# Addresses at multiples of 2048 bytes and two steps moved: a two-layer graph kernel in split fp32 on one NeuronCore

## What is computed

```
x1  = layernorm(x + adj @ (scale * (adj @ (x @ W0))) + bias)
deg1 = row sums of adj, deg2 = row sums of adj.T   (0 replaced by 1)
out = layernorm(x1 + (adj / deg1) @ x1 @ W_in + (adj.T / deg2) @ x1 @ W_out)
scale = sum over levels of d_list * filt * d_list
```

## Time and profile before

| | |
|---|---|
| median of 3 runs | 754.64 us (754.17 to 755.70) |
| profiled execution, its own time | 754.41 us |
| its span, first to last instruction | 752.6 us |
| TensorE busy | 740.1 us, 3337 matmuls |
| VectorE busy | 552.9 us |
| ScalarE busy | 475.0 us |
| mean granted TensorE clock | 0.998 |
| HBM read, written | 205.95 MB, 2.10 MB |

### The profile page before, as it was taken

How to read it: one execution, slowest core, us unless ns; L and a number is a source line. 1 busy time by engine, 2 the same in 40 slices (tenths; PEclk the granted TensorE clock), 3 DMA queues, 4 the chain that set the end, 5 groups by cost and what they waited for, 6 DMA issues and landing times. The chain is left out here.

```text
span 752.6 us, 9059 instructions
## 1 busy us (share of the span) xinstructions
PE 740.1 (98%) x3337; PEld 605.5 (80%) x3337; DVE 552.9 (73%) x673; ACT 475.0 (63%) x1167; POOL 0.2 (0%) x4
## 2 busy tenths in 40 slices
PE   8999999999999999999999999999999999999995
PEld 5878888888888888788888888888887888888884
DVE  4896865838373464787665647988679999899994
ACT  5996673837263543234343446998799888877771
POOL 0000000000000000000000000000000000000000
PEclk9999999999999999999999999999999999999999
DMA  9998875656656445255455459999989999999981
GB/s 325 411 375 342 356 264 214 258 215 209 216 191 223 168 168 224 78 209 207 178 175 217 167 197 373 381 385 381 382 303 371 384 366 373 381 358 336 348 350 29
DMA packets 35532, 208.64 MB, mean 277 GB/s; under 512 B 3616, under 2 KB 8480, under 8 KB 11040
## 3 DMA queue, kind: packets, MB, share of 16 engines
q1 hardware_dynamic: 35072, 207.86, 73.5%
q10 hardware_dynamic: 416, 0.20, 0.1%
HBM read 205.95 MB, written 2.10 MB: 276 GB/s over the span
## 5 line engine op out<-in xcount | busy, mean ns | idle before, releaser
L376 DVE TENSOR_TENSOR lo<-raw,hi 128x2048 fp32r<-128x2048 f32 x184 | 417.0, 2287 | 139.4 <-ACT hi L274 104.6
L274 ACT ACTIVATE hi<-raw 128x512 fp32r<-128x512 f32 x512 | 315.5, 620 | 60.8 <-DMA raw<-in_adjT_b 38.4
L575 PE MATMUL accA<-hi,x_hi 128*128 128x512 f32 x512 | 203.1, 397 | 1.4 <-ACT x_hi L282 0.7
L578 PE MATMUL accA<-hi,x_lo 128*128 128x512 f32 x512 | 200.3, 391 | 0.3 <-DVE x_lo L381 0.3
L277 ACT ACTIVATE hi<-raw 128x2048 fp32r<-128x2048 f32 x64 | 121.7, 1912 | 72.1 <-DMA raw<-in_adjT_b 72.1
L584 PE MATMUL accA<-lo,x_hi 128*128 128x512 f32 x512 | 138.5, 392 | 0.8 <-DVE lo L376 0.8
L575 PEld LDWEIGHTS accA<-hi,x_hi 128*128 128x128 f32 x512 | 96.2, 188 | 23.1 <-ACT hi L274 2.0
L584 PEld LDWEIGHTS accA<-lo,x_hi 128*128 128x128 f32 x512 | 95.9, 188 | 22.8 <-DVE lo L376 1.7
L578 PEld LDWEIGHTS accA<-hi,x_lo 128*128 128x128 f32 x512 | 96.2, 188 | 20.8 <-DVE x_lo L381 0.6
L575 PE MATMUL accB<-hi,v_hi 128*128 128x512 f32 x256 | 101.2, 395 | 0.9 <-DVE turned L433 0.9
L578 PE MATMUL accB<-hi,v_lo 128*128 128x512 f32 x256 | 100.1, 391 | 0.0
(11 more groups left out here) (66 smaller groups left out, 461.4 us busy)
## 6 DMA issues: line engine op xcount, KB each, us to landing
raw<-in_adjT_b SPq DMA_DIRECT2D x127, 1024.0 KB, 4.9
raw<-in_adj_b SPq DMA_DIRECT2D x64, 1024.0 KB, 5.0
rows<-in_xT_b SPq DMA_DIRECT2D x8, 256.0 KB, 9.8
rows<-in_x_t SPq DMA_DIRECT2D x8, 256.0 KB, 5.9
out<-rows SPq DMA_DIRECT2D x7, 256.0 KB, 5.6
raw<-in_adjT_b SPq DMA_DIRECT2D x4, 256.0 KB, 5.0
out<-rows SPq DMA_DIRECT2D x1, 128.0 KB, 1.9
out<-rows ACTq DMA_DIRECT2D x1, 128.0 KB, 1.9
```

The lines of the kernel that those rows point to most:

```text
L274: nc.scalar.activation(hi[slot][:, t], raw[slot][:, t], ACT.Copy, accum_out=sums[:, TPB * K + t, C:C + 1]).then_inc(s_hi, 1)
L376: nc.vector.tensor_tensor(lo[slot][:], raw[slot][:], hi[slot][:], ALU.subtract).then_inc(s_lo, 1)
L575: nc.tensor.matmul(acc, r_hi[:, TPB * K + t], h[:, t], start=(first and t == 0), stop=False)
L578: nc.tensor.matmul(acc, r_lo[:, TPB * K + t], h[:, t], start=False, stop=False)
```

## The change

1. The ring is placed at a multiple of 2048 bytes in place of 64, so it starts at 129,024 and no longer at 131,008. A tensor `unused` of 1920 bytes is put ahead of x_hi, which then starts at 18,432 in place of 16,512; x_lo, v_hi, v_lo, each 16,384 bytes, and all that comes after follow.
2. turn_z(7) on ScalarE and v_block(7) on VectorE are done in iteration N1 and no longer in N1 + 1.
3. In iteration N1 + 3 VectorE does o_sum(6) between x1_block(7) and x1_parts(7).

```diff
+LINE = 4 * BLK
...
-        ring_at = nc.sbuf_top // 64 * 64 - 2 * RING * CHUNK
+        ring_at = nc.sbuf_top // LINE * LINE - 2 * RING * CHUNK
...
+        pair_at = -(-nc.sbuf_base // LINE) * LINE
+        sb("unused", [P, (pair_at - nc.sbuf_base) // 32 * 8])
         x_hi = sb("x_hi", [P, NT, P], F32R)
...
                 if 0 <= I < NB - 1 and n < N1 + 2:
                     turn_z(I)
-                if n == N1 + 1:
+                if n == N1:
                     turn_z(NB - 1)
...
-                if n == N1 + 1:
+                if n == N1:
                     v_block(NB - 1)
                 if n == N1 + 2:
                     o_sum(NB - 1)
                 if n == N1 + 3:
                     x1_block(NB - 1)
+                    o_sum(NB - 2)
                     x1_parts(NB - 1)
-                    o_sum(NB - 2)
```

## The result

The changed kernel takes 747.26 us (median of 5 runs, 746.37 to 748.00) against 754.64 us before (5 runs): a ratio of 0.9901, interval 0.9886 to 0.9915. It is 7.4 us faster, where 1.3 us was forecast, and lies outside the range that was given.

What follows compares the result with a forecast made beforehand. TensorE was taken to bound the kernel nearly everywhere. 754.41 - 1.23 (the wait) - 0.1 (DMA) = 753.1 us from the profiled execution, given as 753.3 because the median is 0.2 higher; range 750.5 to 755.8.

Steps and rivals of the forecast that it cites:

- What bounds the kernel: Whole kernel: TensorE bounds nearly everywhere, busy 740.1 of 752.6 us at full granted clock.
- Part 1: VectorE, iteration N1+3: sum of block 6 ahead of the Newton steps removes TensorE's whole wait of 1.23 us.
- The lead survived: Late DMA-busy stretches: the 1.23 us lead carried in full to the end, since loads follow TensorE's releases; ends 0 and 1.23.
- B: Late loads or waits on lo: the lead is lost there, time 754.3 us; chance 0.09.
- Part 2: turn_z(7) and v_block(7) a chunk sooner: v_block is bound by its data and stays at 287.62, worth 0.
- Part 3: Addresses of ring and x_hi: matmul effect taken as 0, bounded by 16 ns gain and 11 ns loss per matmul.
- the signs that the prediction listed: Right: TensorE busy near 740, 8 matmuls in 1.83 us; wrong: 1.71 to 1.80, above 1.84, or a new wait.
- Rival A: Matmuls get faster, 16 ns each being the price of the 64 bytes: 27.5 us less, 725.6 us; chance 0.11.
- Rival C: Slower: moving and stationary operands at equal offsets modulo 2048 meet in memory, 4.6 us more, 757.7 us; chance 0.08.
- The DMA term: TensorE's early 0.5 us wait for hi: faster landing at the new addresses gains 0 to 0.5 us, taken as 0.1.

Runs made afterwards that it cites:

- the scan: Changed kernel with groups of 24 fp32r matmuls ahead of the work, stationary less moving address d stepped from 0 to 256 bytes, then a bf16 group: 850.9 us.
- the pairs alone: Changed kernel with the ring back at 64 bytes below a multiple of 2048, only x_hi, x_lo, v_hi, v_lo moved: 765.72 us, ratio 1.0144 against before.

## Why the prediction was wrong

- **What bounds the kernel** stood: TensorE, with 98% before and after.
- **Part 1** was right in each step: the sum behind the aggregates, the reciprocal without idle time, the product on time. The moved steps alone gave 1.3 us for a forecast 1.23, with an interval of 0.7 to 2.0 us.
- **The lead survived**, as forecast: the steps-alone run ends 1.3 us sooner. B falls as far as that interval allows.
- **Part 2** was right with 0: 747.02 without the move, 747.26 with it.
- **Part 3 is the step that failed**: "I take 0". It measured 6.4 us. The bounds held (at most 16 ns less, up to 11 ns more per matmul): this change gave -2.2 ns, and one of the two address moves by itself up to +4.4. What was wrong was the choice of the value. I took VectorE's read of the same tiles as the nearest row, but by the experiments the cost isn't in reading one misplaced tile; it hangs on the difference between the two tiles that TensorE reads. The trace had a sign of it that I used only as a spread: starts 0.24 and 0.22 us apart in a stream that waits for nothing. After the change they are even. An even stream isn't yet a fast one, though: in the scan, the matmuls at d = 208 start 232 to 234 ns apart. Of the signs that the prediction listed, only TensorE's busy time (734.6 us, not near 740) spoke clearly; 8 matmuls in 1.82 us lay between the forecast 1.83 and the 1.80 that was to show A.
- **Rival A** had the right direction and the wrong mechanism and size: not the 64 bytes of the moving tile, and not 16 ns but 2.2. It also counted the gain as capped late in the kernel by the DMA; with 2.2 ns there was room for it all the way, 2.2 x 3072 = 6.8 us for 6.4 measured. The gap between 216 and 226.7 ns stays at the best address. The 216 ns that the Trainium skill (TensorE: Matmul & The Clock Gate, Back-to-back issue gap) gives as the gap of a 512-column matmul taken by itself was met by dense bf16 here (215.5) and by no fp32r matmul; the 131 ns that the same section gives for a stream of weight loads and matmuls was met by nothing here.
- **Rival C** named the right pair of reads and had the sign the wrong way round: equal offsets are the best case, and moving one of the two alone costs 10 to 12 us. Its price came from the wrong rows too: with equal offsets the two lines still differ (394 and 390 ns, where it was 397 and 391), so that gap isn't the price of an address. And as the effect repeats after 256 bytes, it falls on every stationary tile of 512 bytes and not on one in four. By the Trainium skill (SBUF — State Buffer, Who interferes with whom) TensorE's two read ports are independent; the scan disagrees, with 227 to 233 ns in the rows above by the difference of the two addresses alone.
- **The DMA term** of 0.1 us can't be told from the scatter of the starts, and no run tried it alone. In the traces of before and after, the packets of 8 KB most often take 309 ns alike, so no dearer landing shows at the old addresses.

What stays open: why the distance is short at 0 and 240, middling at 8, 176 and 192, and long elsewhere. The runs give the curve, not the way in which the memory is divided.

## What to carry to other kernels

Where TensorE is the bound and each matmul loads its own weights in fp32r, look at the distances of starts in a stretch without waits: if they aren't equal, or differ from one kernel to the next, compare the addresses of moving and stationary tiles modulo 256. Keep the difference at 0 for all pairs that are used together, and move both or neither: an alignment of one tensor alone cost 10 to 12 us here, 1.3 to 1.6%. Take the price of a wait from the starts (1.23 us) and not from the list of waits (0.9), which counts from a modelled end; the runs agree with the first but are too coarse to rule out the second. And a step whose data came late gained nothing by an earlier place in its queue.

## What the runs showed of the hardware that was not expected

- The distance of back-to-back fp32r matmuls of 512 columns, each with a weight load of 128, depends on the stationary tile's address less the moving tile's, modulo 256. In the kernel it is 226.7 ns at 0, 228.9 at 192, 232.3 at 128 and 233.3 at 64. In the scan, with every other engine and the DMA idle, it is 227 at 240 and 256, 229 at 192, 230 at 176, 231 at 8, and 233 at 32, 64, 128 and 224.
- Dense bf16 stood at 215.4 to 215.5 ns at the differences shown; bf16 at a stride of 4 bytes at 225.4 to 226.7.
- Halves of an alignment don't add: against the moved steps alone, the ring alone costs 10.1 us and the pairs alone 12.1, and both together give 6.4.
